# Gathered rows in the pooled channels' buffer, four homes for expert outputs, another order for the first five expert tiles

## The chip, the cores and the metric

One Trainium2 chip, one of its cores. The core has five engines with queues of their own: TensorE (PE, matrix products; PEld is its loading of weights), VectorE (DVE), ScalarE (ACT), GpSimd (POOL) and SyncE (SP, which mostly starts transfers). They run side by side and meet only at semaphores; each works through its own instructions in program order. The metric is the device time of one execution in microseconds (us). The clock of TensorE has two levels here, 1.2 and 2.4 GHz; PEclk 0.50 and 1.00 in the rows.

## The reference

`x` is (4, 1024, 192). B = 4 sequences; after the pooling each has N = 512 tokens of D = 192 channels, 2048 tokens in all.

```python
h = pool_max2(relu(pointwise(depthwise_conv7(x))))           # 4 x 512 x 192
h = layernorm(real(fft2(h))) * gamma + beta
n = layernorm(h); q, k, v = n @ Wq.T, n @ Wk.T, n @ Wv.T     # 12 heads of 16
h = h + causal_taylor_attention(q, k, v) @ Wo.T              # weights 1 + s + s*s/2
x2 = layernorm(h)
probs = softmax(x2 @ Wg + bg)                                # 8 experts, the best one each
y = expert_e(x2) = gelu(x2 @ W1[e] + b1[e]) @ W2[e] + b2[e]  # 192 -> 768 -> 192
ffn = y * max(probs)
v = clip(ffn @ Wv + bv); scores = sigmoid(x2 @ Wm + bm)
mask = scores among the 204 highest of its sequence
feats = diag((tridiag(v) - i)^-1) * mask                     # scan along the tokens
out = h + ffn + bk_scale * (feats @ Wo + bo)
```

## The kernel before, in words

The sequences go one after the other through convolution, Fourier transform, projection and attention. Then come the experts. Tokens are sorted by expert into 23 tiles of 128 slots (`SLOT_TILES`), each tile with one expert. The places of the tokens are found in two passes: pass 0 for sequences 0 to 2 while the attention of sequence 3 still runs, pass 1 for sequence 3, whose rows `x2` exist only after its attention is projected and normalised. Pass 0 fills tiles 0 to 4 (`SURE` = 5) for certain; tile 5 and later need pass 1.

One slot tile takes these steps:

- GpSimd `gather(i)` (L619): an indirect transfer brings 128 rows of `x2` from DRAM into `xs[i % 2]`.
- TensorE `turn_slots(i)` (L1640, L1641) transposes them into PSUM; ScalarE `copy_slots(i)` (L766) copies them to `xsT`.
- VectorE `fetch_w1(i)` (L1127, L1128, L1134) copies the expert's first weights (the 768 wide part, the pair part of 384) and its bias out of the tables of all experts. It reads the expert's number with a register load first.
- TensorE `up(i)` (24 products, L1650 and L1654), ScalarE `gelu(i)` (6 activations, L774), TensorE `down(i)` (6 products, shown as 12 records, L1664) into the one bank `att[2]`.
- VectorE `copy_out(i)` takes the result out of `att[2]` (L1148), weighs it (L1151) and sums it with `Wv` (L1154). GpSimd `store_slots(i)` (L629) scatters it to DRAM.

`down(i)` waits until tile i-1 has been taken out of `att[2]` (`ys_copied`), `up(i)` until `xsT` is copied (`xst_copied`) and gelu i-2 is done. The outputs have two homes `ys`; `copy_out(i)` waits until tile i-2 is stored.

Around the seam between attention and experts, TensorE's order is written by hand: `find_tokens(0)` (L1564), `turn_attended` (L1488, L1490), `turn_back` (L1409, L1413), `output` of the last sequence (L1421, L1424), with short groups of idle products between them (`keep_clock`, L1346), then slot tiles 0 and 1, the turning of x2 (`turn`, L1550), `down(0)`, `logits` (L1574), and so on up to a loop over pairs of tiles that begins with `up(5)`. The second pass on VectorE is `choose(1)` (L980 to L990), `place(1)` (L1003 to L1060), `name_tiles(1)` (L1100 to L1104: experts of the tiles, `te_ready`) and `name_slots(1)` (L1069 to L1075: token of each slot, `slots_named`).

`xs`, `ys` and `hT` share the buffer `probs`, whose first 768 columns also hold the attention result that `turn_back` reads. So `gather(0)` waits for `back_done`:

```python
if i == 0:
    pool.wait_ge(s_saved, 32 * (B - 1))
    pool.wait_ge(slots_named, 1)
    pool.wait_ge(back_done, 2 * B)
```

## Time and profile before

| | us |
|---|---|
| median of 3 runs | 426.69 |
| the runs | 425.43 to 428.47 |
| profiled execution, its own time | 426.79 |
| its span, first to last instruction | 425.0 |

| engine | busy us | share of the span |
|---|---|---|
| PE | 379.0 | 89% |
| DVE | 281.1 | 66% |
| ACT | 160.5 | 38% |
| POOL | 103.0 | 24% |

The chain that ended last runs over PE for 57% of the span and over DVE for 24%. By time the run has these parts: convolution to the last attention, 0 to about 255 us; the seam with the first expert tiles, 255 to 304 us; the loop over expert tiles, 304 to about 383 us; the scan, the features and the stores, to 425 us. A share over the whole span says little here: the change touches only the second part, and there the question is what each engine waits for.

In the rows, the start is in us from the beginning of the span, then the duration; a bracket is the idle time ahead and what ended it. `issue` there stands for time for which the profile shows no releaser. Several like instructions in a row are merged, with their count.

### The profile page before, as it was taken

Reading aid. Unit: us, or ns where it says so; the run is one execution under the profiler, and the core shown is the slowest. Engines: PE = TensorE matmul, PEld = TensorE weight load, DVE = VectorE, ACT = ScalarE, POOL = GpSimd, SP = SyncE. Lnnn points to the kernel's source line nnn. Section 1 sums busy time; section 2 is a strip of 40 time slices with the busy share of each in tenths; the row PEclk is TensorE's granted clock in tenths of the full one; section 3 lists DMA queues with packets and bytes.
Section 4 is the critical chain, followed back from the end, with each engine's and each line's share of the span. In section 5 each row is a group of like instructions: output and inputs, shape, how many; then the busy total and the mean of one; then the engine's idle time right before and its main releaser. Section 6 shows DMA issues by size and latency. Waiting matters only on the chain.

```text
span 425.0 us, 7812 instructions
## 1 busy us (share of the span) xinstructions
PE 379.0 (89%) x2658; PEld 255.4 (60%) x2659; DVE 281.1 (66%) x901; ACT 160.5 (38%) x321; POOL 103.0 (24%) x154
## 2 busy tenths in 40 slices
PE   8999899799998998989998899995899999997273
PEld 4476547133673364723677228894899999996252
DVE  4589734899688995986433853664446656657783
ACT  1001131595317843187531781471243443441000
POOL 2000030151303612045300260310543443421000
PEclk9999899699999999999995799997899999999656
DMA  8664049400685015810279705310411112112504
GB/s 266 194 197 149 0 123 258 126 3 2 191 217 149 2 38 155 217 52 2 68 209 291 333 20 202 129 35 9 164 43 56 45 53 56 43 40 54 169 1 148
DMA packets 26900, 47.94 MB, mean 113 GB/s; under 512 B 11044, under 2 KB 21860, under 8 KB 25332
## 3 DMA queue, kind: packets, MB, share of 16 engines
q1 hardware_dynamic: 21412, 32.73, 25.0%
q10 hardware_dynamic: 2288, 7.15, 6.4%
q0 software_dynamic: 3168, 7.65, 6.2%
q8 instruction: 17, 0.28, 0.3%
q14 instruction: 15, 0.12, 0.1%
HBM read 36.84 MB, written 10.68 MB: 112 GB/s over the span
## 4 chain that ended last, share of the span: by engine, by line
PE 57%; DVE 24%; DMA 6%; issue 5%; ACT 4%; POOL 2%; DVEq 1%; SPq 0%; ACTq 0%; POOLq 0%
PE att L1664 10%; PE ring L1650 8%; PE ring L1654 5%; PE att L1527 4%; PE ring L1515 4%; ACT probs L674 3%; DMA w1b<-q_parts 3%; DVE wide L824 2%; PE att L1490 2%; POOL probs L603 2%; PE att L1581 2%; PE ring L1395 1%; PE ring L1361 1%; DVE stats L833 1%; PE ring L1400 1%
## 5 line engine op out<-in xcount | busy, mean ns | idle before, releaser
L674 ACT ACTIVATE probs<-ring,ones 128x1024 f32<-128x1024 f32 (+2 forms) x72 | 66.3, 970 | 15.9 <-PE ring L1515 14.5
L603 POOL TENSOR_SCALAR_AFFINE_SELECT probs<-probs 128x256 f32<-128x256 f32 (+1 forms) x72 | 40.7, 569 | 111.6 <-ACT probs L674 111.4
L1664 PE MATMUL att<-w,probs 128*128 x276 | 50.6, 335 | 3.3 <-DVE probs L1148 3.3
L1664 PEld LDWEIGHTS att<-w,probs 128*128 128x128 f32 x276 | 45.8, 195 | 4.2 <-issue 4.1
L1515 PE MATMUL ring<-w1b 128*128 128x512 bf16 (+3 forms) x192 | 40.6, 324 | 6.5 <-ACT probs L674 3.6
L824 DVE SCALAR_TENSOR_TENSOR wide<-w,wdw,wide 128x512 f32<-128x512 f32 x60 | 44.1, 779 | 0.8
L1527 PE MATMUL att<-probs,va 128*32 128x512 f32 (+3 forms) x384 | 39.8, 454 | 2.4 <-POOL probs L603 1.8
L629 POOL DMA_INDIRECT ffn_by_token<-probs,target_i x23 | 23.1, 1002 | 52.6 <-DVE probs L1154 44.7
L1515 PEld LDWEIGHTS ring<-w1b 128*128 128x128 bf16 x192 | 13.1, 101 | 37.8 <-ACT probs L674 26.5
L774 ACT ACTIVATE probs<-ring,q_area 128x128 f32<-128x128 f32 x72 | 19.9, 375 | 38.1 <-DVE k_area L1127 13.5
L619 POOL DMA_INDIRECT probs<-x_by_token,source_i x23 | 22.6, 984 | 41.4 <-issue 16.7
L1148 DVE TENSOR_TENSOR probs<-att,oT 128x192 f32<-128x192 f32 x23 | 8.2, 358 | 31.8 <-PE att L1664 30.0
L774 ACT ACTIVATE probs<-ring,k_area 128x128 f32<-128x128 f32 x66 | 18.2, 375 | 26.3 <-PE ring L1654 23.7
L467 POOL DMA_DIRECT2D k_parts<-k_area x12 | 6.9, 578 | 82.3 <-ACT k_area L707 77.7
L1346 PE MATMUL att<-idle 128*128 128x256 bf16 x172 | 25.0, 314 | 1.2 <-POOL idle L578 1.2
L1346 PEld LDWEIGHTS att<-idle 128*128 128x128 bf16 x172 | 19.0, 113 | 7.8 <-issue 2.9
L1527 PEld LDWEIGHTS att<-probs,va 128*32 128x32 f32 x384 | 8.2, 108 | 22.3 <-POOL probs L603 18.1
L1650 PE MATMUL ring<-xsT,q_area 128*128 128x128 f32 x144 | 19.2, 285 | 1.7 <-issue 1.7
L1650 PEld LDWEIGHTS ring<-xsT,q_area 128*128 128x128 f32 x144 | 17.4, 196 | 2.7 <-issue 2.1
L1650 PE MATMUL ring<-xsT,k_area 128*128 128x128 f32 x132 | 17.4, 282 | 0.6 <-ACT xsT L766 0.6
L1650 PEld LDWEIGHTS ring<-xsT,k_area 128*128 128x128 f32 x132 | 15.6, 191 | 1.9 <-issue 0.8
L857 DVE TENSOR_REDUCE pooled<-ring 128x512 f32<-128x1024 f32 x4 | 4.9, 1226 | 17.7 <-PE ring L1365 12.9
(369 smaller groups left out, 713.7 us busy)
## 6 DMA issues: line engine op xcount, KB each, us to landing
w1b<-k_parts ACTq DMA_DIRECT2D x16, 384.0 KB, 9.8
w1b<-q_parts SPq DMA_DIRECT2D x16, 384.0 KB, 9.1
w<-in_w SPq DMA_DIRECT2D x1, 4608.0 KB
w1a<-in_w1a SPq DMA_DIRECT2D x1, 3072.0 KB, 10.3
w<-in_x SPq DMA_DIRECT2D x4, 512.0 KB, 3.5
w<-in_x SPq DMA_DIRECT2D x8, 256.0 KB, 5.0
q_parts<-q_area SPq DMA_DIRECT2D x12, 128.0 KB, 2.6
k_parts<-k_area POOLq DMA_DIRECT2D x12, 128.0 KB, 2.6
```

Of the source, the lines that this page charges most:

```text
L603: nc.gpsimd.affine_select(diag, diag, [[0, len(UNITS[n][1])], [1, P]], ALU.is_ge, minus_one, base=0, channel_multiplier=-1).then_inc(p_rea ...
L619: nc.gpsimd.indirect_dma_start(xs[slot], None, known, bass.IndirectOffsetOnAxis(source_i[:, i:i + 1], 0)).then_inc(s_xs[slot], 16)
L629: nc.gpsimd.indirect_dma_start(ffn_dram, bass.IndirectOffsetOnAxis(target_i[:, i:i + 1], 0), ys[slot], None).then_inc(s_ys[slot], 16)
L674: nc.scalar.activation(squares(n), bank[:, :, 0:N - P * j], ACT.Square, bias=ones[:, 0:1], scale=0.25).then_inc(sq_done, 1)
L774: nc.scalar.activation(hT[slot][:, c, :], ring[slot][:, c % 2, P * (c // 2):P * (c // 2) + P], ACT.Gelu_apprx_tanh, bias=b1_col[slot][:, c ...
L824: ins = nc.vector.scalar_tensor_tensor(dst, src, w, dst, ALU.mult, ALU.add)
L1346: nc.tensor.matmul(bank[:, 0:2 * P], idle[:, 0:P], idle[:], start=True, stop=True)
L1515: last = nc.tensor.matmul(bank[:, at, 0:N - P * j], k_stack[:, h, P * j:P * j + P], q_stack[:, h, P * j:N], start=True, stop=True)
L1527: last = nc.tensor.matmul(att[g][QUAD * q:QUAD * q + QUAD, P * j:N], va[:, j, h, :], squares(n)[:, at, :], start=(j == 0), stop=(j == 1))
L1650: nc.tensor.matmul(out[c], w1_wide[slot][:, P * c:P * c + P], xsT[slot][:, 0, :], start=(c < 2), stop=False)
L1654: last = nc.tensor.matmul(out[c], w1_pair[slot][rows, P * (c // 2):P * (c // 2) + P], xsT[slot][rows, 1, :], start=False, stop=(c >= HC - 2))
L1664: last = nc.tensor.matmul(att[2][:, 0:D], hT[slot][:, c, :], w2[:, bass.ds((e * HC + c) * D, D)], start=(c == 0), stop=(c == HC - 1))
```

## The change

- `xs`, the gathered rows, moves from `probs` to `pooled`, the buffer of the pooled channels, which is free once the last Fourier transform is done. `gather(0)` now waits for `row_done` in place of `back_done`. `ys` has four homes (`YS`), each with its own semaphore; `hT`, behind them in `probs`, begins 386 columns further on.
- TensorE: slot tiles 0 and 1 are turned ahead of `output`; of 14 idle products around `output`, 2 are left, ahead of it. Tiles 2 and 3 are turned ahead of x2 (`turn`), each before or behind an `up`. `down(2)` moves ahead of `up(4)`, `down(3)` and `down(4)` ahead of the transpose of the scores; tiles 5 and 6 go up before `down(5)`, and the loop starts one pair later.
- VectorE: `first_weights()` fetches the wide weights and the biases of tiles 0 and 1 during the last attention, ahead of `name_slots(0)`; only the pair parts stay where all was. `copy_out` is cut in `take_out` (the copy out of PSUM, L1148 before) and `weigh_out` (L1151, L1154). Tile 1 is taken out, and tile 4's bias fetched, in the middle of `place(1)`; tile 2 directly behind it; `name_slots(1)` comes ahead of `name_tiles(1)`, tile 3 is taken out behind both. The weighing of 1 to 3 and the copy of the scores come later, between the fetches for tiles 5 and 6.
- ScalarE: tiles 2 and 3 are copied ahead of `gelu(1)`; tile 4 is copied ahead of `gelu(3)`, and `gelu(4)` and tile 5 follow ahead of its loop.
- GpSimd: `gather(5)` and `gather(6)` come directly behind `store_slots(0)`.

```diff
-        xs = [probs[:, 2 * P * i:2 * P * i + 2 * P] for i in range(2)]
+        xs = [pooled[:, i, 0:2 * P] for i in range(2)]
         at = 2 * 2 * P
-        ys = [probs[:, at + (D + 1) * i:at + (D + 1) * (1 + i)] for i in range(2)]
-        at += 2 * (D + 1)
+        ys = [probs[:, at + (D + 1) * i:at + (D + 1) * (1 + i)] for i in range(YS)]
+        at += YS * (D + 1)
...
+        def outs_stored(eng, tiles):
+    for i in range(YS):
+        eng.wait_ge(s_ys[i], 16 * len(range(i, tiles, YS)))
...
-            pool.wait_ge(back_done, 2 * B)
+            pool.wait_ge(row_done, B)
...
     for i in range(SURE):
         gather(i, i % 2)
     pool.wait_ge(s_vzero, 16)
-    for i in range(SLOT_TILES):
-        store_slots(i, i % 2)
+    store_slots(0)
+    gather(SURE, SURE % 2)
+    gather(SURE + 1, (SURE + 1) % 2)
+    store_slots(1)
+    for i in range(2, SLOT_TILES):
+        store_slots(i)
         if i + SURE < SLOT_TILES:
             gather(i + SURE, (i + SURE) % 2)
...
     copy_slots(0, 0)
     copy_slots(1, 1)
     gelu(0, 0)
+    copy_slots(2, 0)
+    copy_slots(3, 1)
     gelu(1, 1)
     turned(B - 1)
-    copy_slots(2, 0)
-    copy_slots(3, 1)
     exponents(1)
     nc.scalar.activation(score[:], lg[:, :, E], ACT.Sigmoid).then_inc(sc_ready, 1)
     gelu(2, 0)
-    with act.Fori(1, TILE_PAIRS - 1) as i:
+    copy_slots(4, 0)
+    gelu(3, 1)
+    gelu(4, 0)
+    copy_slots(5, 1)
+    with act.Fori(2, TILE_PAIRS - 1) as i:
...
             name_tiles(0)
+            first_weights()
             name_slots(0)
...
         st.then(V.tensor_tensor(tile_of(excl), tile_of(excl), wide_e(here), ALU.add))
+        if halfway is not None:
+            halfway()
         pre = misc[:, 2 * P:2 * P + w].rearrange("p (t e) -> p t e", e=E)
...
+    def first_weights():
+        dve.wait_ge(te_ready, 1)
+        dve.wait_ge(s_w1a, 16)
+        dve.wait_ge(s_part_out[0], 16 * 2 * PARTS * B)
+        dve.wait_ge(s_part_out[1], 16 * 2 * PARTS * B)
+        for i in range(2):
+            fetch_wide(i, i, expert_of(i))
+        for i in range(2):
+            fetch_bias(i, i, expert_of(i))
...
+    def take_out(i):
+        e = expert_of(i)
+        ahead(dve, s_ys[i % YS], 16 * (i // YS))
         dve.wait_ge(dn_done, i + 1)
-        out = ys[slot][:, 0:D]
+        out = ys[i % YS][:, 0:D]
         V.tensor_tensor(out, att[2][:, 0:D], b2[:, bass.ds(e * D, D)], ALU.add
                         ).then_inc(ys_copied, 1)
+
+    def weigh_out(i):
+        out, v = ys[i % YS][:, 0:D], ys[i % YS][:, D:D + 1]
...
     dve.wait_ge(s_w1b, 16)
-    fetch_w1(0, 0)
-    fetch_w1(1, 1)
+    for i in range(2):
+        fetch_pair(i, i, expert_of(i))
     add_attended(B - 1)
     normalise_again(B - 1)
     fetch_w1(2, 0)
     fetch_w1(3, 1)
     dve.wait_ge(s_w2, 32)
-    copy_out(0, 0, 0)
+    copy_out(0)
     choose(1)
     fetch_w1(4, 0, bias=False)
-    place(1)
+
+    def second_out():
+        take_out(1)
+        fetch_bias(4, 0, expert_of(4))
+
+    place(1, second_out)
+    take_out(2)
+    name_slots(1)
     name_tiles(1)
-    name_slots(1)
-    fetch_bias(4, 0, dve.value_load(te_i[0:1, bass.ds(4, 1)], min_val=0, max_val=E - 1))
+    take_out(3)
     dve.wait_ge(te_ready, 2)
-    for i in range(1, SLOT_TILES - 1):
-        copy_out(i, i % 2, i // 2)
-        if i > 1 and i + 3 < SLOT_TILES:
+    fetch_w1(5, 1)
+    weigh_out(1)
+    weigh_out(2)
+    fetch_w1(6, 0)
+    weigh_out(3)
+    dve.wait_ge(st_done, 1)
+    V.tensor_copy(score_t[:], misc[0:TT, 2 * P:3 * P]).then_inc(st_copied, 1)
+    st.then(V.memset(qq[:, 0:2, :, :, :], 0.0))
+    st.mark(V.memset(qq[:, 1, :, 0, 0:1], 1.0))
+    st.mark(V.memset(qq[:, 0, :, 0, 1:2], 1.0))
+    st.mark(V.memset(neg_pos[:, 0:1], -GROUP_SCALE))
+    st.mark(V.memset(neg_pos[:, 1:2], GROUP_SCALE))
+    for i in range(4, SLOT_TILES - 1):
...
     turn_attended(B - 1)
-    keep_clock(6, ring[1][:, 0, :])
+    keep_clock(6)
     turn_back(B - 1)
-    keep_clock(6, ring[1][:, 0, :])
-    output(B - 1)
-    keep_clock(8, ring[0][:, 1, :])
...
-        pe.wait_ge(w1_fetched, 3 * i + 2)
+        pe.wait_ge(w1_fetched, 5 + i if isinstance(i, int) and i < 2 else 3 * i + 2)
...
     turn_slots(0, 0, 1)
     turn_slots(1, 1, 1)
+    keep_clock(2)
+    output(B - 1)
     up(0, 0)
+    pe.wait_ge(attn_added, B)
+    turn_slots(2, 0, 2)
     up(1, 1)
-    pe.wait_ge(attn_added, B)
+    turn_slots(3, 1, 2)
+    pe.wait_ge(xst_copied, 4)
     turn(B - 1)
     pe.wait_ge(te_ready, 1)
     pe.wait_ge(s_w2, 32)
     down(0, 0)
     pe.wait_ge(t2_copied, B)
-    turn_slots(2, 0, 2)
-    turn_slots(3, 1, 2)
     logits(B - 1)
     up(2, 0)
     count(1)
     down(1, 1)
     up(3, 1)
     turn_slots(4, 0, 3)
+    down(2, 0)
     up(4, 0)
     find_tokens(1)
+    down(3, 1)
+    down(4, 0)
     pe.wait_ge(sc_ready, 1)
     pe.wait_ge(slots_named, 2)
     nc.tensor.transpose(misc[0:TT, 2 * P:3 * P], score[:], ident[:]).then_inc(st_done, 1)
-    down(2, 0)
-    down(3, 1)
     pe.wait_ge(te_ready, 2)
     turn_slots(5, 1, 3)
-    with pe.Fori(2, TILE_PAIRS - 1) as i:
+    up(5, 1)
+    turn_slots(6, 0, 4)
+    up(6, 0)
+    turn_slots(7, 1, 4)
+    down(5, 1)
+    with pe.Fori(3, TILE_PAIRS - 1) as i:
```

How the instructions stand on three engines follows; the line number at the start of a row is that of its own kernel.

TensorE at the seam, from the idle products behind `turn_attended` to the first `up`; `pooled` and, of before, `probs` with `ident` into `ring1` are the slot tiles, `wo` the projection. Before:

```order
L1346 MATMUL ring1<-idle 128x256 x6
L1409 MATMUL ring0<-ident,probs 128x128 x4
L1413 MATMUL ring0<-ident,probs 64x128 x4
L1346 MATMUL ring1<-idle 128x256 x6
L1421 MATMUL att<-wo,probs 128x192 x4
L1424 MATMUL att<-wo,probs 128x192 x4
L1346 MATMUL ring0<-idle 128x256 x8
L1640 MATMUL ring1<-ident,probs 128x128
L1641 MATMUL ring1<-ident,probs 128x128
L1640 MATMUL ring1<-ident,probs 128x128
L1641 MATMUL ring1<-ident,probs 128x128
L1650 MATMUL ring0<-xsT0,q_area 128x128 x6
```

And now:

```order
L1392 MATMUL att<-idle 128x256 x6
L1455 MATMUL ring0<-ident,probs 128x128 x4
L1459 MATMUL ring0<-ident,probs 64x128 x4
L1683 MATMUL ring1<-ident,pooled 128x128
L1684 MATMUL ring1<-ident,pooled 128x128
L1683 MATMUL ring1<-ident,pooled 128x128
L1684 MATMUL ring1<-ident,pooled 128x128
L1392 MATMUL att<-idle 128x256 x2
L1467 MATMUL att<-wo,probs 128x192 x4
L1470 MATMUL att<-wo,probs 128x192 x4
L1693 MATMUL ring0<-xsT0,q_area 128x128 x6
L1697 MATMUL ring0<-xsT0,q_area 128x128 x6
```

The two slot tiles moved ahead of the projection, and `up(0)` follows it at once.

ScalarE from the table load for gelu on; `xsT0` and `xsT1` are the copies of even and odd slot tiles, `x2T` the turned x2, `probs<-ring` a gelu. Before:

```order
L766 ACTIVATE xsT0<-ring1 128x256
L766 ACTIVATE xsT1<-ring1 128x256
L774 ACTIVATE probs<-ring0,q_area 128x128 x6
L774 ACTIVATE probs<-ring1,k_area 128x128 x6
L755 ACTIVATE x2T<-att 96x1024
L766 ACTIVATE xsT0<-att 128x256
L766 ACTIVATE xsT1<-att 128x256
L747 ACT_TABLE_LOAD
```

And now:

```order
L773 ACTIVATE xsT0<-ring1 128x256
L773 ACTIVATE xsT1<-ring1 128x256
L781 ACTIVATE probs<-ring0,q_area 128x128 x6
L773 ACTIVATE xsT0<-att 128x256
L773 ACTIVATE xsT1<-att 128x256
L781 ACTIVATE probs<-ring1,k_area 128x128 x6
L762 ACTIVATE x2T<-att 96x1024
L754 ACT_TABLE_LOAD
```

The copies of tiles 2 and 3 moved ahead of `gelu(1)` and of `x2T`.

VectorE in the second pass; `te_i` with the ISA rows behind it is the register load of an expert's number. Before, the end of that stretch, with `name_slots(1)`, the bias of tile 4 and the taking out of tile 1:

```order
L1072 TENSOR_SCALAR source_i<-held 128x18
L1073 SCALAR_TENSOR_TENSOR spare_row<-held,dump_tab 128x18
L1075 SCALAR_TENSOR_TENSOR target_i<-held,spare_row 128x18
L1194 TENSOR_LOAD te_i
L1194 ISA x2
L1134 ISA
L1134 COPY q_area<-b1t 128x6
L1144 TENSOR_LOAD te_i
L1144 ISA x2
L1148 ISA
L1148 TENSOR_TENSOR probs<-att,oT 128x192
```

And now the middle of `place(1)`:

```order
L1045 TENSOR_TENSOR excl<-excl,et 128x32
L1138 TENSOR_LOAD te_i
L1138 ISA x2
L1184 ISA
L1184 TENSOR_TENSOR probs<-att,oT 128x192
L1138 TENSOR_LOAD te_i
L1138 ISA x2
L1166 ISA
L1166 COPY q_area<-b1t 128x6
L1049 TENSOR_TENSOR key<-excl,misc 128x32
```

The taking out of tile 1 and the bias moved between the two halves of `place(1)`.

## Rows read from the trace of the kernel before

**Rows 1.** Stretches of the run: busy time per engine, PEclk, DMA share and GB/s.
```profile
79.00:80.00 1.00, 0.59 (x2) 0.13 (x2) 0.86 (x5) 1.00 (x2) 0.40 (x1) 0.50 1.00 393
...
230.00:235.00 5.00, 3.82 (x17) 2.91 (x17) 1.71 (x7) 1.11 (x1) 0.35 (x1) 0.50 1.01 356
...
291.00:292.00 1.00, 1.00 (x11) 1.00 (x12) 0.00 (x0) 0.00 (x0) 0.00 (x0) 0.50 0.00 0
...
305.00:350.00 45.00, 45.00 (x375) 41.59 (x373) 25.29 (x82) 18.93 (x70) 19.94 (x21) 1.00 0.18 52
```
**Rows 2.** Chain of work that ended last: start, us, engine, line.
```profile
313.83 1.44 PE ring L1650 x12
```
**Rows 3.** Timeline, TensorE: start, us, operation, count, [idle before and its releaser].
```profile
77.54 1.34 PE L1515 MATMUL ring<-w1b 128*128 128x512 bf16 x4 [2.08 <-DMA w1b<-q_parts]
...
267.60 1.05 PE L1346 MATMUL ring<-idle 128*128 128x256 bf16 x8
...
269.87 1.50 PE L1650 MATMUL ring<-xsT,q_area 128*128 128x128 f32 x12
...
272.17 1.60 PE L1650 MATMUL ring<-xsT,k_area 128*128 128x128 f32 x12
...
274.57 1.08 PE L1550 MATMUL att<-ident,x_all 128*96 128x128 f32 x8
275.49 2.12 PE L1664 MATMUL att<-w,probs 128*128 x12
...
277.88 1.85 PE L1574 MATMUL misc<-wgm,x2T 96*128 96x9 f32 x16
...
288.91 2.13 PE L1650 MATMUL ring<-xsT,q_area 128*128 128x128 f32 x12 [1.71 <-issue]
...
296.98 3.69 PE L1664 MATMUL att<-w,probs 128*128 x12 [1.82 <-DVE probs L1148]
```
**Rows 4.** Timeline, ScalarE, from the last projection's copy to gelu 3.
```profile
264.38 0.81 ACT L689 ACTIVATE probs<-ring 128x768 f32<-128x768 f32 x1 [8.30 <-PE ring L1413]
...
266.50 0.20 ACT L761 ACTIVATE warm<-ones 128x1 f32<-128x1 f32 x1
...
286.88 1.65 ACT L774 ACTIVATE probs<-ring,k_area 128x128 f32<-128x128 f32 x6 [1.63 <-PE ring L1654]
288.39 0.42 ACT L766 ACTIVATE xsT<-att 128x256 f32<-128x256 f32 x1
```
**Rows 5.** Timeline, VectorE, from the first slot table to the second output.
```profile
258.35 0.20 DVE L1067 COPY held<-misc 128x46 f32<-128x46 f32 x1 [7.97 <-PE misc L1564]
...
265.10 0.56 DVE L1127 COPY k_area<-w1a 128x768 f32 x1
...
273.81 0.15 DVE L953 COPY nz<-x_all 128x1 f32<-128x1 f32 x1
...
285.61 0.21 DVE L1035 TENSOR_TENSOR key<-excl,misc 128x32 f32<-128x32 f32 x1
...
289.49 0.34 DVE L1100 TENSOR_TENSOR y<-te,et 1x192 f32<-1x192 f32 x1
...
290.44 0.16 DVE L1104 TENSOR_SCALAR te_i<-te 1x19 int32<-1x19 f32 x1
...
294.56 0.18 DVE L1075 SCALAR_TENSOR_TENSOR target_i<-held,spare_row 128x18 int32<-128x18 f32 x1
...
296.47 0.36 DVE L1148 TENSOR_TENSOR probs<-att,oT 128x192 f32<-128x192 f32 x1 [0.97 <-issue]
```
**Rows 6.** Timeline, GpSimd: attention's masks, first gather, gather of tile 5.
```profile
252.34 0.64 POOL L603 TENSOR_SCALAR_AFFINE_SELECT probs<-probs 128x512 f32<-128x512 f32 x1 [0.39 <-ACT probs L674]
...
265.20 1.36 POOL L619 DMA_INDIRECT probs<-x_by_token,source_i  x1 [10.66 <-PE ring L1413]
...
295.49 0.98 POOL L619 DMA_INDIRECT probs<-x_by_token,source_i  x1 [14.84 <-issue]
```
**Rows 7.** Gathers of 255 to 310 us, start to landing, minimum, median, maximum.
```profile
DMA to landing us min/median/max: 2.7/2.8/2.9
```

53 lines of the change are left out of this document (24 added, 29 removed).

## The prediction

> **What bounds the kernel now.** I first read the windows by stage. In the loop over expert tiles TensorE is busy 45.00 of 45 us at full clock, VectorE 25.29 [rows 1]. The change alters no instruction inside that loop but the addresses of `xs`, `ys` and `hT`, so the loop keeps its length, and I ask only when it reaches a common point. The chain has one: `up(7)` begins at 313.83 [rows 2], with all `up` to 6 and all `down` to 5 behind it. In the changed order `up(7)` is the first operation of the loop, with the same work behind it. Whatever this point gains, the end gains.
>
> Ahead of it, TensorE's timeline shows the price of one operation [rows 3]: `up` 2.30 us (269.87 to 272.17), `turn` 0.92 (274.57 to 275.49), `down(0)` with two slot tiles 2.39 (275.49 to 277.88), which is 1.95 and twice 0.22, logits 1.7. A row's own duration overlaps the next by about 0.15. From `up(0)` at 269.87 to `up(7)` at 313.83 are 43.96 us. The work in it is 7 `up` (16.1), 6 `down` (11.7), 6 slot tiles (1.3), `turn`, logits and small products (4.1): 33.2 us. So 10.8 us are idle time and half clock: 1.71 ahead of `up(4)` and 1.82 ahead of `down(2)` are two of the gaps, and `down(2)` takes 3.69 in place of 2.12 [rows 3].
>
> **The change step by step**, on the clock of the profiled run.
>
> *Gathers.* The slot table is begun at 258.35 and takes four dependent operations of 0.2 [rows 5]: ready at 259.1. `gather(0)` now needs nothing more. Tile 5's gather began 0.75 after its table (294.74 to 295.49) [rows 5, 6], so it starts at 259.85 in place of 265.20, and lands 2.8 later [rows 7], at 262.7; the second follows 1.66 behind (1.36 plus 0.3) and lands at 264.3. TensorE ends `turn_back` at about 264.35, when ScalarE's copy begins (264.38) [rows 4]. The slot tiles fit there (to 264.8), since `output` has to wait for that copy until 265.19 anyway. What is queued behind a late gather now is `output`, and behind that x2: the cover is 0.4 us, after it each late microsecond counts in full.
>
> *Up(0).* The eight idle products behind `output` began at 267.60, `up(0)` came at 269.87, after a wait for the second gather [rows 3]. Now it starts at 267.6: ScalarE ends its table load and trial at 266.70 [rows 4] and copies tile 0 by 267.1. Gain 2.3.
>
> *To x2.* `up(0)` to 269.9, slot tile 2, `up(1)` to 272.4, slot tile 3 to 272.65. Then `turn` waits for x2, whose last operation VectorE does at 273.81, to 273.96 [rows 5]. Nothing in the change moves it. `turn` starts at 274.1, before 274.57: of the 2.3 us, 0.46 are left, and TensorE has a new gap of 1.45 us. As two slot tiles are out of the way, the logits end 0.9 earlier, at 278.7.
>
> *Second pass.* VectorE is 0.9 earlier up to the middle of `place(1)`: 284.7 in place of 285.61 [rows 5]. There the change adds `take_out(1)` (0.36), tile 4's bias (0.17) and a register load for each. The load's price has no row of its own; the nearest is the gap of 0.97 ahead of `copy_out(1)` [rows 5], which may hold waits too. Bounds 0 and 0.97; I take 0.6, nearer to the row. That is 1.7 us, and the second half of `place(1)` is 3.9 (285.61 to 289.49) [rows 5]: positions at 290.4, before 289.5. The operations of 1 to 3 that are cut out come back later; they are hidden, as `down` of tile 4 waits only for taking out.
>
> *Tiles 2 to 4.* TensorE: `up(2)` to 281.0, count to 281.5, `down(1)` to 283.5, `up(3)` to 285.8, slot tile 4 to 286.0, `down(2)` to 288.0, `up(4)` to 290.3. Before, `up(4)` waited 1.71 for a copy that stood behind `gelu(3)`: ScalarE did that gelu from 286.88 and the copy from 288.39 to 288.81 [rows 4]. Now the copy stands ahead of the gelu and `down(2)` fills the time. `find_tokens(1)` waits for positions to 290.6 and takes 0.9; `down(3)` to 293.5. VectorE names slots by 292.4, tiles by 293.6 (1.1, from 289.49 to 290.60) [rows 5], takes out tile 3 by 294.55 with one register load. `down(4)` runs 294.7 to 296.7, after a gap of 1.2.
>
> *Tiles 5 to 7.* `gather(5)` starts 0.75 after 292.4 and lands by 296.0, hidden. Slot tile 5 is turned at 296.9 and copied by 297.5; `up(5)` 297.7 to 300.0, slot tile 6 to 300.2. `up(6)` now stands directly behind, and its copy behind `gelu(5)`: 1.65 for the gelu and 0.42 for the copy [rows 4], so it starts at 302.3, a gap of 2.1. `up(6)` to 304.6, slot tile 7 and `down(5)` to 306.8, `up(7)` at 306.95. That is 6.9 us ahead of 313.83: 2.3 ahead of `up(0)` and 4.6 out of the 10.8, of which 6.1 remain.
>
> *First weights ahead of time.* Two wide copies of 0.56 and two small ones fall into the 7.97 us in which VectorE waited for the slot table [rows 5]. If that cover were gone, about 3 us of them with register loads would stand ahead of `gather(0)`. They lie beside the last masks on GpSimd. The first gather's instruction, beside such copies (265.10), took 1.36; tile 5's, with VectorE still, 0.98 [rows 5, 6]. So a mask may take 0.4 longer, 0.8 for two; each had 0.39 idle ahead of it [rows 6], so I take 0 and keep 0.8 for the range. The Trainium skill, "SBUF — State Buffer", section "Who interferes with whom", says that VectorE in its two-port mode and GpSimd fully block one another; the two rows bear it out in direction. By the skill's rule each wide copy would hold a mask for up to its 0.56, 1.1 us in all, and the time would be 422.6.
>
> *Four homes.* No store is waited for before, by these rows. Nothing is won in the loop.
>
> *The clock.* TensorE fell to half clock in the three cases here in which it had idled so long: 2.08 ahead of 77.54, and 0.50 at 79; 1.71 ahead of 288.91, and 0.50 at 291; 1.82 ahead of `down(2)`, which then took 3.69 [rows 1, 3]. The new gap of 2.1 ahead of `up(6)` is of that kind. A stay at half clock costs what `down(2)` shows, 3.69 less 2.12, 1.6 us; an `up` shows 2.13 for 1.50 in its first half [rows 3], so 1.3 for both. The gap of 1.45 is shorter than these three, but `turn` and logits follow. I count one fall: 6.9 less 1.6 is 5.3, and 426.79 less 5.3 is 421.5. The profiled execution (426.79) stands 0.1 above the median, so this needs no shift. The Trainium skill, "TensorE: Matmul & The Clock Gate", section "HAM oscillation — how this bites in real kernels", would have only longer gaps than these do harm. By that the 2.1 us gap costs nothing, which is the first rival; the rows of this trace speak against it.
>
> **The rivals.** *No fall of the clock*: 419.9. For it, before lost one stay to a gap of 1.71 and one to 1.82, and the clock may look at a luckier moment; against it, three of three gaps.
>
> *Two falls*: also after 1.45 us. `down(0)`, the logits and `up(2)` then run slowly; one stay costs 1.6, and two in a row, if the logits don't lift it, 3. It gives 423.1 to 424.5. For it: at 230 to 235 the clock was still 0.50 with TensorE busy 3.82 of 5 us [rows 1].
>
> *VectorE becomes the limit of tiles 2 to 4*: each register load costs 0.97 in place of 0.6, and the loads stand on the way to the slot table and to `down(4)`. Four of them add 1.5, in all 423.0.
>
> *The change doesn't do what it says*: the early gathers are worth 0.66 of waiting, x2 comes when it came, and what the new order fills on TensorE comes back as waits for gelu and for taking out. Then 0.46 remains: 426.3.
>
> *Slower*: the clock falls at the 1.45 us gap and stays low through the sparse stretch up to the loop, as it did from about 225 to past 235 [rows 1]. From 276 to 302, 3 `up` more at 1.3 and 4 `down` more at 1.6, 1.9 for the logits and 0.5 for the rest make about 13 less what hides in the gaps (2), so 11: 6.9 are lost and 4 more, near 431. It decides once half clock lasts some 15 us.
>
> **How the numbers follow.** Forecast 0.38, no fall 0.15, two falls 0.25, VectorE 0.09, no effect 0.07, slower 0.06. The likeliest is 421.5, with its own range 420.3 to 422.6 (masks 0.8 and register loads up, shorter gaps down). From no fall, with 0.6 below it, to two falls with 0.5 above: 419.3 to 425.0; outside are the last two cases and a part of the edges. Over 1% is 4.27 us, about what a measurement of this kernel can tell from no change. Faster than that, under 422.4: no fall, nine tenths of the forecast and a little of two falls, 0.56. Slower than 431.0: half of the last case and other harm not named, 0.05. The rest, 0.39, is within 1%.
>
> **What would show it.** `up(0)` within 0.3 us of the end of `output`; x2's last operation at the same time; a gap of about 1.4 us ahead of `turn`, about 2 ahead of `up(6)` and 0.50 behind it; `up(4)` at full clock directly behind `down(2)`; slot table two at about 292.4; `up(7)` near 308.5. The sum is wrong if `output` waits for the slot tiles, if the masks stretch the last attention, or if the loop's period changes.

## The result

| | before | changed |
|---|---|---|
| median of 20 runs, us | 428.76 | 425.71 |
| the runs, us | 425.43 to 432.63 | 423.22 to 430.99 |
| profiled execution, its own time | 426.79 | 424.41 |
| its span | 425.0 | 422.5 |
| changed to before, 95% interval | | 0.9946 (0.9925 to 0.9967) |

The changed kernel is 0.5% faster, 2.3 us (1.4 to 3.2 by the interval). The medians of all runs lie 3.05 us apart; the ratio is formed from fast runs alone, without the few in the slower state that executions on this chip can fall into. Forecast were 421.5 us and 5.3 us of gain. Two things hide in the difference. The three runs of before that the forecast started from were low ones: the median of 20 is 2.1 us above theirs. And of the gain, more than half is missing; where it went is the question of the rest.

How the parts of the two executions stand, from the start of `find_tokens(0)` on TensorE to the starts of `up(0)`, `up(7)` and `up(22)`, the last tile's, and to the end, in us:

| | before | changed |
|---|---|---|
| `find_tokens(0)` to `up(0)` | 14.5 | 12.2 |
| `up(0)` to `up(7)` | 43.8 | 44.2 |
| `up(7)` to `up(22)` | 69.0 | 68.9 |
| `up(22)` to the end | 42.3 | 42.4 |

I call the first two together *the seam*: 58.3 before, 56.4 changed. The loop and what follows kept their length. In the seam the time up to `up(0)` fell by the 2.3 forecast, and nothing came of the 3.0 more (4.6 less 1.6 of half clock) that was to come behind it; that part is even 0.4 longer.

TensorE of the changed kernel in the seam (timeline; the line numbers are its own: L1470 is the end of `output`, L1693 and L1697 are `up`, L1683 and L1684 a slot tile, L1596 `turn`, L1707 `down`; the last row is the beginning of `up(7)`, cut off by the edge of the view), which answers to [rows 3]:

```profile
266.17 0.92 PE L1470 MATMUL att<-wo,probs 64*128 64x192 f32 x8
267.02 1.60 PE L1693 MATMUL ring<-xsT,q_area 128*128 128x128 f32 x12
...
273.50 1.05 PE L1596 MATMUL att<-ident,x_all 128*96 128x128 f32 x8 [1.06 <-ACT xsT L773]
...
287.81 1.50 PE L1693 MATMUL ring<-xsT,q_area 128*128 128x128 f32 x12
...
291.03 2.20 PE L1707 MATMUL att<-w,probs 128*128 x12
294.15 2.21 PE L1707 MATMUL att<-w,probs 128*128 x12 [0.93 <-DVE probs L1184]
...
297.21 1.58 PE L1693 MATMUL ring<-xsT,k_area 128*128 128x128 f32 x12 [0.52 <-issue]
298.72 0.94 PE L1697 MATMUL ring<-xsT,k_area 64*128 64x128 f32 x12
...
299.76 0.27 PE L1684 MATMUL att<-ident,pooled 128*128 128x128 f32 x1
304.06 2.90 PE L1693 MATMUL ring<-xsT,q_area 128*128 128x128 f32 x12 [4.03 <-DVE k_area L1166]
306.89 1.65 PE L1697 MATMUL ring<-xsT,q_area 64*128 64x128 f32 x12
308.47 0.47 PE L1683 MATMUL att<-ident,pooled 128*128 128x128 f32 x1
...
311.23 0.94 PE L1693 MATMUL ring<-xsT,k_area 128*128 128x128 f32 x7
```

Up to 299.76 it goes as forecast: `up(0)` right behind `output`, a gap of 1.06 ahead of `turn`, `up(4)` at full clock behind `down(2)`, a gap of 0.93 ahead of `down(4)`, `up(5)` 0.52 behind its slot tile. Then come 4.03 us of nothing ahead of `up(6)` where 2.1 were forecast, and behind it `up(6)` takes 4.4 us (304.06 to 308.47) in place of 2.4, and `down(5)` is stretched too.

The releases show that the gap is not ScalarE's doing alone. ScalarE in that stretch (timeline; L781 is gelu, L773 the copy of a slot tile):

```profile
296.73 0.38 ACT L773 ACTIVATE xsT<-att 128x256 f32<-128x256 f32 x1 [4.51 <-issue]
302.03 1.66 ACT L781 ACTIVATE probs<-ring,k_area 128x128 f32<-128x128 f32 x6 [4.91 <-remote]
303.54 0.42 ACT L773 ACTIVATE xsT<-att 128x256 f32<-128x256 f32 x1
```
VectorE's and GpSimd's first instructions behind the gap (L1142 is the copy of the next weights, L622 the next gather):

```profile
302.13 0.56 DVE L1142 COPY k_area<-w1a 128x768 f32 x1 [1.11 <-remote]
302.31 1.24 POOL L622 DMA_INDIRECT pooled<-x_by_token,source_i  x1 [1.24 <-remote]
```
The granted clock around it (windows, columns as in [rows 1]):

```profile
302.00:303.00 1.00, 0.00 (x0) 0.00 (x0) 0.83 (x2) 0.97 (x4) 0.69 (x1) 0.88 1.00 328
306.00:309.00 3.00, 3.00 (x20) 2.55 (x20) 0.00 (x0) 0.36 (x2) 0.00 (x0) 0.50 0.00 1
309.00:310.00 1.00, 1.00 (x6) 1.00 (x6) 0.00 (x0) 1.00 (x6) 0.57 (x1) 0.70 0.00 0
```

`gelu(5)` waits for the last product of `up(5)`, whose record ends at 299.66, and begins at 302.03, with `remote` as its releaser: the wait ended with a signal that belongs to no record ending near it. VectorE's copy of the next weights (302.13) and GpSimd's next gather (302.31), which wait for `up(5)` and for slot tile 6, go on within 0.3 us of it, after 1.11 and 1.24 of idle time marked `remote`. The trace also holds the times of the signals themselves. That of `up(5)` is recorded at 302.00 and that of slot tile 6 at 302.05, 2.34 and 2.02 us after the ends of the products' records (299.66, 300.03); of the 309 signals of TensorE in this trace the median comes 0.01 after its record. So all three engines got TensorE's signals some 2 us late by the records. I call these *the late signals*. The ends of TensorE's records are modelled by the profile, so whether the products themselves ended late or only their signals is not shown. The mean clock of 0.88 in 302 to 303 and of 0.70 in 309 to 310 puts the fall at 302.8 and the rise at 309.6: 6.8 us at half clock.

### The profile page after: what moved, and what is told of

Same layout as the page of the kernel before. It is cut to its first block and busy times, and to the rows that moved or that the text cites. A ratio compares the mean times of both kernels' runs of the same rounds, so it can differ in the third digit from the quotient of the medians.

```text
span 422.5 us, 7775 instructions
## 1 busy us (share of the span) xinstructions
PE 374.3 (89%) x2642; PEld 252.8 (60%) x2647; DVE 281.7 (67%) x901; ACT 160.3 (38%) x321; POOL 103.3 (24%) x154
## 5 line engine op out<-in xcount | busy, mean ns | idle before, releaser
L1707 PE MATMUL att<-w,probs 128*128 x276 | 49.5, 330 | 1.8 <-DVE probs L1184 1.7
L1707 PEld LDWEIGHTS att<-w,probs 128*128 128x128 f32 x276 | 44.7, 192 | 2.8 <-issue 2.7
L1561 PE MATMUL ring<-w1b 128*128 128x256 bf16 (+3 forms) x188 | 39.5, 321 | 7.5 <-ACT probs L681 3.5
L781 ACT ACTIVATE probs<-ring,q_area 128x128 f32<-128x128 f32 x72 | 19.9, 374 | 31.7 <-PE ring L1697 13.5
L622 POOL DMA_INDIRECT pooled<-x_by_token,source_i x23 | 22.9, 993 | 36.8 <-issue 20.6
L781 ACT ACTIVATE probs<-ring,k_area 128x128 f32<-128x128 f32 x66 | 18.2, 376 | 26.5 <-PE ring L1697 19.0
L1392 PE MATMUL att<-idle 128*128 128x256 bf16 x180 | 25.9, 310 | 1.2 <-POOL idle L581 1.2
L1693 PE MATMUL ring<-xsT,q_area 128*128 128x128 f32 x144 | 20.0, 292 | 4.0 <-DVE k_area L1166 4.0
L1693 PEld LDWEIGHTS ring<-xsT,q_area 128*128 128x128 f32 x144 | 18.3, 203 | 5.1 <-issue 4.5
L1693 PE MATMUL ring<-xsT,k_area 128*128 128x128 f32 x132 | 17.2, 280 | 0.5 <-issue 0.5
L1693 PEld LDWEIGHTS ring<-xsT,k_area 128*128 128x128 f32 x132 | 15.7, 191 | 1.6 <-issue 0.7
```

The costliest lines, as they stand in the source:

```text
L622: nc.gpsimd.indirect_dma_start(xs[slot], None, known, bass.IndirectOffsetOnAxis(source_i[:, i:i + 1], 0)).then_inc(s_xs[slot], 16)
L781: nc.scalar.activation(hT[slot][:, c, :], ring[slot][:, c % 2, P * (c // 2):P * (c // 2) + P], ACT.Gelu_apprx_tanh, bias=b1_col[slot][:, c ...
L1392: nc.tensor.matmul(bank[:, 0:2 * P], idle[:, 0:P], idle[:], start=True, stop=True)
L1561: last = nc.tensor.matmul(bank[:, at, 0:N - P * j], k_stack[:, h, P * j:P * j + P], q_stack[:, h, P * j:N], start=True, stop=True)
L1693: nc.tensor.matmul(out[c], w1_wide[slot][:, P * c:P * c + P], xsT[slot][:, 0, :], start=(c < 2), stop=False)
L1707: last = nc.tensor.matmul(att[2][:, 0:D], hT[slot][:, c, :], w2[:, bass.ds((e * HC + c) * D, D)], start=(c == 0), stop=(c == HC - 1))
```

## The experiments

Each kernel's own seam, from its trace, is the measure, since the totals scatter more. The time to the start of `find_tokens(0)` varied from 253.2 to 260.3 us over twenty traces of code that is the same up to there but for the first weights. The first 250 us show what goes with it, TensorE's granted clock (the column behind the busy times). The changed kernel unchanged, in its last trace (`again_e`):

```profile
0.00:250.00 250.00, 229.37 (x1542) 125.72 (x1543) 180.20 (x512) 104.31 (x146) 55.39 (x105) 0.96 0.48 138
```
And with a later store of the scores (`scores_late`):

```profile
0.00:250.00 250.00, 226.73 (x1476) 124.69 (x1481) 175.68 (x497) 98.74 (x139) 54.40 (x98) 0.94 0.47 138
```

By my estimate 0.96 against 0.94 of 250 us is 5 us of clock, and the starts of `find_tokens(0)` were 253.7 and 260.3. A difference of 2 us between two single times says nothing about an edit behind it.

### The changed kernel again, three variants of the place ahead of up(6)

Run unchanged:

> The changed kernel once more, so that the variants below have a partner on the same chip. Its first trace has up(6) at 304.06, 4.03 us after slot tile 6, and ScalarE, VectorE and GpSimd all go on at 302.0 to 302.3 although TensorE's records of up(5) end at 299.66. Theory A (belongs to this order of work): the stop comes again within 0.3 us, ratio to before 0.994. Theory B (an accident of one execution): the gap ahead of up(6) is 2.1 us, and the ratio nearer 0.99.

It gave 424.28 us (median of 4), ratio 0.9885 (0.9807 to 0.9963), and a seam of 53.06 us in place of 56.44: 5.3 us less than before, which is the forecast gain to a tenth. The interval of these 4 runs holds the first ratio too, so it is the trace that tells them apart. A later trace (`again_e`, below) has the same course; TensorE in it:

```profile
296.13 1.58 PE L1693 MATMUL ring<-xsT,k_area 128*128 128x128 f32 x12 [0.52 <-issue]
...
300.65 1.79 PE L1693 MATMUL ring<-xsT,q_area 128*128 128x128 f32 x12 [1.70 <-issue]
302.37 1.65 PE L1697 MATMUL ring<-xsT,q_area 64*128 64x128 f32 x12
...
306.81 1.50 PE L1693 MATMUL ring<-xsT,k_area 128*128 128x128 f32 x12
```
ScalarE of the same trace:

```profile
298.63 1.65 ACT L781 ACTIVATE probs<-ring,k_area 128x128 f32<-128x128 f32 x6 [2.59 <-PE ring L1697]
300.14 0.42 ACT L773 ACTIVATE xsT<-att 128x256 f32<-128x256 f32 x1
```
And its windows with the granted clock:

```profile
301.00:302.00 1.00, 1.00 (x10) 1.00 (x10) 0.27 (x2) 0.00 (x0) 0.69 (x2) 0.94 0.79 295
303.00:304.00 1.00, 1.00 (x11) 0.78 (x9) 0.00 (x0) 0.00 (x0) 0.00 (x0) 0.50 0.83 293
305.00:306.00 1.00, 1.00 (x7) 1.00 (x7) 0.00 (x0) 1.00 (x4) 0.90 (x1) 0.86 0.08 31
```

Here `gelu(5)` (298.63) begins when `up(5)` ends, the gap ahead of `up(6)` (300.65) is 1.70, and by the windows half clock lasts from 301.9 to 305.3, 3.4 us. So the missing 3.35 us of the first trace are two terms: 2.33 more of gap, and 1.0 more of half clock, since the longer stay covers all of `up(6)` and reaches into `down(5)` (`up(6)` to `up(7)` is 7.17 there, 6.16 here).

ScalarE copies slot tile 6 ahead of `gelu(5)`:

```diff
             copy_slots(5, 1)
-            with act.Fori(2, TILE_PAIRS - 1) as i:
+            copy_slots(6, 0)
+            gelu(5, 1)
+            gelu(6, 0)
+            copy_slots(7, 1)
+            with act.Fori(3, TILE_PAIRS - 1) as i:
```

> ScalarE copies slot tile 6 ahead of gelu(5), in place of behind it, and its loop begins one pair later. Theory A (order): what is lost ahead of up(6) is ScalarE's gelu and copy and the half clock behind the gap: up(6) comes within 0.7 us of slot tile 6 and at full clock, up(7) 4 to 5 us earlier, ratio to before 0.984. Theory B (signals of TensorE are held up by something else for 2.3 us at this time): up(6) still comes 2.5 us or more after slot tile 6, half clock stays, ratio about 0.99.

421.36 us, ratio 0.9842 (0.9753 to 0.993), seam 50.33. Against the unchanged kernel beside it (53.06) that is 2.7 us; the 4 to 5 expected were reckoned from the first trace, with its late signals. Its second run is shown below.

TensorE does 14 idle products in the gap, begun when tile 4 has been taken out:

```diff
             turn_slots(6, 0, 4)
+            pe.wait_ge(ys_copied, 5)
+            keep_clock(14)
             up(6, 0)
```

> 14 idle products (1.5 us) are put into the gap ahead of up(6), behind the taking out of tile 4. Theory A (clock): up(6) takes 2.3 in place of 4.4 us and down(5) 1.95, so up(7) comes 2 to 2.7 us earlier at the same start of up(6); ratio 0.989. Theory B (the gap alone counts, or the idle products end too soon): up(6) stays at 4.4 us, ratio 0.994.

421.52 us, ratio 0.9833 (0.9762 to 0.9903), seam 51.6. The same kernel in a later trace, `warm_gap_b`:

> Idle products of TensorE in the gap ahead of up(6), which begin when take_out of tile 4 has been copied. Without late signals 51.6 us as once before. With them: if the signals are late because TensorE itself stands still, the idle products stand still too and the way is about 2.3 us longer, 53.9 us, with or without a half clock behind; if only the signals' way is held up, the products run through and the clock stays at 2.4 GHz.

```profile
299.60 1.58 PE L1693 MATMUL ring<-xsT,k_area 128*128 128x128 f32 x12 [0.52 <-issue]
...
302.14 0.27 PE L1684 MATMUL att<-ident,pooled 128*128 128x128 f32 x1
302.69 1.70 PE L1392 MATMUL att<-idle 128*128 128x256 bf16 x14 [0.28 <-DVE probs L1184]
304.23 1.50 PE L1693 MATMUL ring<-xsT,q_area 128*128 128x128 f32 x12
```

Single time 421.91 us, seam 51.55. `up(6)` stands where it stood within 0.1 us, 4.63 behind `up(5)`, but runs its first half in 1.50; the stay at half clock is gone and `up(6)` to `up(7)` is 4.53 in place of 6.16. So a fall of the clock behind a gap of 1.7 us costs 1.5 to 1.6, as the forecast took it from `down(2)` of before, and it was the gap that brought it. The Trainium skill, "TensorE: Matmul & The Clock Gate", section "HAM oscillation — how this bites in real kernels", lets only longer gaps than this do harm; no trace here with a gap of 1.70 us ahead of `up(6)` was spared (seven), and both with idle products in it were.

The store of the scores, which is on its way while `up(5)` runs, held back until `up(7)`:

```diff
             sp.wait_ge(st_copied, 1)
+            sp.wait_ge(up_done, 8)
```

> SyncE holds back the store of the scores and their spreading to all partitions (1 MB) until up(7) is done. Theory A (these transfers hold up the signals): ScalarE begins gelu(5) at once behind up(5), the gap ahead of up(6) is 2.1 in place of 4.0 us, ratio 0.990. Theory B (they don't): the gap stays 4.0, ratio 0.994 or a little more, if the count of higher scores now waits.

426.59 us, ratio 0.9952 (0.9915 to 0.999), seam 53.07. The second and third trace, with their expectations:

> The changed kernel with the store of the scores held back until up(7), for a second trace. If the score store, which is on its way while up(5) runs, is what delays TensorE's signals, there is no late signal here either and the way from find_tokens(0) to up(7) is 53.1 us again. If the late signals come whatever the scores do, there is a good half chance of 56.4 us.

> The score store held back until up(7), on this chip. Two traces of it on a chip without late signals say nothing on the cause. If this chip shows them in the unchanged kernel (56.4 us): the theory that the score store, which is under way at that moment, delays TensorE expects none here and 53.1 us; the rival (TensorE's own stop at this place of the program) expects 56.4 us again. On a chip without late signals both expect 53.1 us. From up(7) to up(22) 72.1 us rather than 68.9 as in both traces, since the comparisons of the scores then start later.

Seams 53.11 and 53.06. All three are without the late signals, but so were all other kernels that ran beside them. The edit has a price of its own, 3.2 us: from `up(7)` to `up(22)` all three traces take 72.1 to 72.2 us, not 68.9. TensorE of `scores_late_c` shows where:

```profile
318.84 2.21 PE L1708 MATMUL att<-w,probs 128*128 x12 [2.88 <-DVE probs L1185]
```
VectorE of the same trace:

```profile
317.40 0.75 DVE L1173 TENSOR_SCALAR_CACHE_REDUCE y<-wide,score 128x512 f32<-128x512 f32 x1 [5.96 <-DMA wide<-scores_linear]
...
318.23 0.36 DVE L1185 TENSOR_TENSOR probs<-att,oT 128x192 f32<-128x192 f32 x1
```

VectorE waits 5.96 us for the scores to come back from DRAM, the taking out of tile 7 (L1185, 318.23) is queued behind, and TensorE stands 2.88 us ahead of its next `down`. The store in its early place is thus needed.

### The gather's wait put back

```diff
-                    pool.wait_ge(row_done, B)
+                    pool.wait_ge(back_done, 2 * B)
```

> One part undone alone: the first gather waits for back_done again, as before, but TensorE's order stays as changed, with slot tiles 0 and 1 ahead of the projection. Theory A (the early gather is what makes the new order possible, and its cover is small): both gathers land 3.4 to 5.2 us behind turn_back, the projection waits for them from 264.8 on, x2 and all behind it come about 4.5 us later; ratio to the kernel before 1.003. Theory B (the gathers don't matter, x2 comes when it came): no change, ratio 0.992.

It ran beside two runs of before and one of the changed kernel:

> The kernel before once more, for a second trace. So far the changed kernel's three traces have 53.1, 53.1 and (with the stop) 56.4 us from the first product behind the attention, find_tokens(0), to up(7); the one trace of before has 58.3. Theory A (the stage gained what was forecast, 5.3, and the whole lost some elsewhere): before again has 57.8 to 58.8 in that stage, and what differs lies ahead of find_tokens(0). Theory B (the first trace of before was unlucky in its clock): the stage takes 55 to 57 here.

> A third trace of the kernel before, for the same question, above all for when the last attention ends: 255.4 in the first trace; the changed kernel's traces have 254.8 to 260.3. Theory A (the masks or the early weights make the attention end later): about 255.4 again. Theory B (this point moves by some us from execution to execution in both kernels): anything from 254 to 261.

> The changed kernel, one more trace: 53.1 us from find_tokens(0) to up(7) and a gap of 1.9 us ahead of up(6), if the stop of the first trace was an accident; 56.4 and 4.0 if it is common.

429.37 us, ratio 1.0041 (0.9995 to 1.0087). TensorE at the seam:

```profile
261.55 0.66 PE L1459 MATMUL ring<-ident,probs 128*64 128x128 f32 x8
265.93 0.33 PE L1683 MATMUL ring<-ident,pooled 128*128 128x128 f32 x1 [3.72 <-DMA pooled<-x_by_token,source_i]
...
267.21 0.48 PE L1683 MATMUL ring<-ident,pooled 128*128 128x128 f32 x1 [0.84 <-DMA pooled<-x_by_token,source_i]
...
268.12 2.63 PE L1467 MATMUL att<-wo,probs 128*128 128x192 f32 x8
```

The transfers now land 3.72 and 0.84 us after TensorE is ready, `output` is queued behind them, and its first half takes 2.63 in place of 1.57. From `find_tokens(0)` to `up(0)` it is 18.3 in place of 12.2, and the seam 61.27 against 56.45 of `again_b` on the same chip: 4.8 worse, and 3 worse than before. Up to `up(0)` it is 6.1 worse; 1.2 come back behind the gap of 4.06 ahead of `up(6)`, where this trace stays at half clock for 3.4 us and not for 6.8 (`up(6)` to `up(7)` 5.93, not 7.16). Both traces have the late signals, which before has not, and the interval of the ratio holds 1. So the new order on TensorE pays only with the rows in `pooled`; without them its gain is gone, and whether it would be a loss is not shown.

`again_b` took 425.05 us and has the late signals (seam 56.45), and `gather_late` has them too. The two runs of before took 432.08 and 427.18 us with seams of 61.19 and 58.44. In the first the stay at half clock that begins in the gap ahead of `down(2)` lasts 10.2 us, where the other three traces of before have 3.4, without any edit; so before can lose there as well.

### The first weights put back

```diff
                     name_tiles(0)
-                    first_weights()
                     name_slots(0)
...
             divide(B - 1)
+            first_weights()
             dve.wait_ge(s_w1b, 16)
```

> The changed kernel, but VectorE brings the first two wide weight halves and biases after the last division again, not among the masks. In the changed kernel that block ran from 249.84 to 253.64, 3.8 us. Placed behind the division (end 262.7) it would end at about 265.9, the two narrow halves about 1.8 us later at 267.8; up(0), which started at 267.02, needs the first narrow half (about 267.0), so it moves by 0 to 0.2; add_attended, which started at 267.14, moves to 267.8, and the turn of x2 with it. Theory (the early weights are worth what they take off this path): about 0.7 us slower than the changed kernel from find_tokens(0) to up(7). Rival (the block in front cost as much ahead of the attention's end, where it delayed the masks): the attention ends up to 3.8 us earlier and the whole is 1 to 3 us faster than the changed kernel. Second rival (nothing hangs on it): the same within 0.3 us.

422.36 us, ratio 0.9919 (0.9876 to 0.9963); seam 53.62 against 53.05 of the unchanged kernel beside it (`again_c`). The 0.57 us are 0.1 ahead of `up(0)` and the gap ahead of `turn`, 1.54 in place of 1.06. The clock did not fall behind this longer gap either; TensorE (timeline):

```profile
272.96 1.05 PE L1596 MATMUL att<-ident,x_all 128*96 128x128 f32 x8 [1.54 <-issue]
```

The block is worth 0.6 us behind the attention, near the 0.7 expected. The contention that the forecast kept 0.8 us for is there, and it fell on both engines in turn. In the changed kernel, VectorE (timeline):

```profile
250.85 0.95 DVE L1142 COPY q_area<-w1a 128x768 f32 x1 [1.05 <-issue]
251.72 0.55 DVE L1142 COPY k_area<-w1a 128x768 f32 x1
```
And GpSimd's masks beside it:

```profile
250.75 0.63 POOL L606 TENSOR_SCALAR_AFFINE_SELECT probs<-probs 128x512 f32<-128x512 f32 x1 [0.39 <-ACT probs L681]
251.77 0.99 POOL L606 TENSOR_SCALAR_AFFINE_SELECT probs<-probs 128x512 f32<-128x512 f32 x1 [0.39 <-ACT probs L681]
```

The first wide copy began behind a mask and took 0.95 instead of 0.55, while that mask took the 0.63 it takes elsewhere. The second wide copy took its 0.55, and the mask that began 0.05 behind it took 0.99. The Trainium skill, "SBUF — State Buffer", section "Who interferes with whom", would have the two engines block one another; the rows agree in size, and each time the one that began later waited. It cost nothing here: `find_tokens(0)` begins 3.02 us after this last long mask in all twenty traces, with a mask of 0.99 as with one of 0.64, such as `weights_late` and the kernel before have.

### Is it the execution, the order or the chip?

> The changed kernel, unchanged, for one more trace of the gap ahead of up(6). Of three traces so far two have TensorE's signals of up(5) about 2.3 us late, a gap of 4.0 us and a way of 56.4 us from find_tokens(0) to up(7), and one has none, a gap of 1.9 us and 53.1 us. The theory that the late signals are a matter of the execution expects one or the other of these two values, nothing between.

424.28 us, seam 53.05, no late signals.

> The kernel with ScalarE's copy of slot tile 6 ahead of gelu(5), once more, to narrow its interval. If the order of ScalarE at this place is what TensorE waited for, the ratio to the kernel before is again 0.984 (0.975 to 0.993) and the way from find_tokens(0) to up(7) again near 50.3 us. If the first result was a lucky execution, the ratio lies near that of the changed kernel, 0.9946, and the way near 53 to 56 us.

419.94 us, ratio 0.9883 (0.9828 to 0.9937), seam 50.33. TensorE in it:

```profile
300.09 0.27 PE L1688 MATMUL att<-ident,pooled 128*128 128x128 f32 x1
300.88 1.58 PE L1697 MATMUL ring<-xsT,q_area 128*128 128x128 f32 x12 [0.52 <-issue]
...
305.49 0.71 PE L1697 MATMUL ring<-xsT,k_area 128*128 128x128 f32 x4
```

(The last row is cut off by the edge of the view.) Gap 0.52, no fall. The 2.73 us that it gains on 53.06 are 1.18 of gap and 1.55 of clock.

> The changed kernel unchanged, with five rounds. Of its order at up(5) there are eight traces from one chip, none with late signals of TensorE, and two from another chip, both with them (again_b, gather_late); the way from find_tokens(0) to up(7) is 53.06 us in the first and 56.45 in the second. Theory (the late signals go with the chip): on a chip without them the way is 53.06 us and the ratio to the kernel before is 1 - 5.3/428 = 0.988 (0.985 to 0.991); on a chip with them 56.45 and 1 - 1.9/428 = 0.9955 (0.993 to 0.998). Rival (they go with the single execution): both values in traces of one chip, and a ratio between.

425.87 us, ratio 0.9964 (0.9928 to 1.0), seam 56.39, late signals.

> The kernel with ScalarE's copy of slot tile 6 ahead of gelu(5), beside the one above on the same chip. Without late signals the way is 50.33 us as twice before. On a chip with them the theory has TensorE's signals of up(5) late here too: the copy of slot tile 6 then waits, up(6) starts about 2.3 us later with a gap near 2.9 us instead of 0.5, a half-clock window follows (1.7 us and more), and the way is 53 to 56 us; against the changed kernel it would still gain about 1 to 3 us.

424.21 us, ratio 0.9928 (0.9888 to 0.9967), seam 53.92. The late signals hit this order too: 2.31 and 1.98 us behind the ends of the records. TensorE:

```profile
301.76 0.27 PE L1688 MATMUL att<-ident,pooled 128*128 128x128 f32 x1
304.52 2.51 PE L1697 MATMUL ring<-xsT,q_area 128*128 128x128 f32 x12 [2.49 <-issue]
```
ScalarE of the same trace:

```profile
304.04 0.39 ACT L773 ACTIVATE xsT<-att 128x256 f32<-128x256 f32 x1 [4.92 <-remote]
304.32 1.65 ACT L781 ACTIVATE probs<-ring,k_area 128x128 f32<-128x128 f32 x6
```

ScalarE begins the copy of slot tile 6, which was turned at 302.0, at 304.04 (`remote`), the gap is 2.49 and half clock follows. Against the changed kernel on the same chip it still gains 2.5 us by the seams.

> The changed kernel once more, to tell of which kind this chip is. With late signals of TensorE after up(5) (two of three chips so far) the gap ahead of up(6) is 4.0 us and the way from find_tokens(0) to up(7) 56.4 us; without them 1.7 to 1.9 us and 53.06 us.

420.44 us, seam 53.09, no late signals, on the chip on which `again_d` and `copy6_c` had them.

> The kernel before on this chip. Of the same stage 58.3 and 58.4 us so far (61.2 in one trace with two more half-clock windows), without a late signal of TensorE. The theory that the late signals belong to the changed order expects 58.3 to 58.4 here on a chip of either kind.

428.03 us, seam 58.20.

All together, with the sets of kernels that ran one after the other on a chip, the seams of their traces, and what these seams would make of the ratio (1 plus the seam less the 58.3 of before, and 3.2 more for the late store, over 428.3, about the median of before). Where a kernel was timed, a set has 4 to 20 runs of it; each kernel of a set has one trace:

| set, chip | late signals | kernel | seam | ratio by the seam | ratio measured |
|---|---|---|---|---|---|
| 1 | yes | changed | 56.44 | 0.9957 | 0.9946 (0.9925 to 0.9967) |
| 2, chip 4 | no | changed | 53.06 | 0.9878 | 0.9885 (0.9807 to 0.9963) |
| | | copy ahead | 50.33 | 0.9814 | 0.9842 (0.9753 to 0.993) |
| | | idle products | 51.6 | 0.9844 | 0.9833 (0.9762 to 0.9903) |
| | | scores late | 53.07 | 0.9953 | 0.9952 (0.9915 to 0.999) |
| 3, chip 12 | yes | changed | 56.45 | | |
| | | gather late | 61.27 | 1.0069 | 1.0041 (0.9995 to 1.0087) |
| 4, chip 4 | no | changed | 53.05 | | |
| | | weights late | 53.62 | 0.9891 | 0.9919 (0.9876 to 0.9963) |
| | | copy ahead | 50.33 | 0.9814 | 0.9883 (0.9828 to 0.9937) |
| 5, chip 1 | yes | changed | 56.39 | 0.9955 | 0.9964 (0.9928 to 1.0) |
| | | copy ahead | 53.92 | 0.9898 | 0.9928 (0.9888 to 0.9967) |
| 6, chip 1 | no | changed | 53.09 | | |
| | | idle products | 51.55 | | |

In a set, either every trace of the new order has the late signals or none has: five traces with, eleven without, no exception. Chip 1 had a set of each kind, so it is not the chip alone. The timed runs bear it out as far as their intervals reach (one of the ten leaves out what the seam says, and only just): the changed kernel's three timed sets stand near 0.988 without and 0.995 to 0.996 with. The order with the copy ahead tells it more plainly: medians of 421.36 and 419.94 us without, 424.21 with, while before had 428.01, 428.28 and 428.05 in the same sets.

What differs between the sets I do not know. An instruction fetch it is not: none is recorded between `up(5)` and `up(6)`, in traces of either kind. The store of the scores is neither ruled out nor shown to be the cause. Its packets were through 1.0 us after its issue in both kinds of traces, and its three traces with the later place fell into sets without late signals. But SyncE, which waits for that store's own signal, issued its next transfer 1.50 to 1.67 us after it in four of the five traces with late signals (1.37 in `copy6_c`), and 1.36 to 1.42 in the eleven without. So the hold-up reaches beyond TensorE. In the first trace (SyncE; 1.37 between the same two in `again_e`):

```profile
298.84 0.33 SPq L551 DMA_DIRECT2D scores_linear<-score_t  x1
300.51 0.35 SPq L557 DMA_DIRECT2D wide<-scores_linear  x1
```

And the two kinds of sets differ in one thing more, of both kernels. The traces of sets 1, 3 and 5 hold 4716 to 4748 signals, those of 2, 4 and 6 hold 5062 to 5068; up to 250 us they hold 3006 to 3050, whatever the kind, and the missing ones, most of them signals of transfers, lie behind. Every trace of the new order with the fewer signals has the late ones, no trace with the full number has. Whether what delays the signals also loses records, or the recording itself delays them, is open. The four traces of before, three of them with the fewer signals, have no late signal at this place. No trace with the idle products fell into a set with late signals.

## Why the prediction was right or wrong

- **The loop keeps its length; what `up(7)` gains the end gains**: right. 68.9 against 69.0, and 42.4 against 42.3.
- **Gathers early, cover 0.4 us, `up(0)` right behind `output`, 2.3 us**: right. The first gather began at 259.27, `up(0)` at 267.02, 0.85 behind the start of `output`'s last part. Its undoing cost 4.8.
- **x2 doesn't come earlier, so only 0.46 is kept at `turn`**: right. `turn` came at 273.50; the profiled execution of changed ran 0.6 earlier from the start of the seam, so this is 274.1 on the clock of the forecast. The gap was 1.06, not 1.45, since the two `up` and two slot tiles ahead of it took 5.4 us (267.02 to 272.44) and not 5.05.
- **No fall of the clock behind this gap**: right, in every trace, even behind the 1.54 us of `weights_late`.
- **Second pass with register loads at 0.6**: right within the bounds; VectorE's two cut-in operations have 0.78 and 0.41 us idle ahead of them, 0.6 in the mean:

```profile
285.19 0.36 DVE L1184 TENSOR_TENSOR probs<-att,oT 128x192 f32<-128x192 f32 x1 [0.78 <-DVE excl L1045]
285.96 0.17 DVE L1166 COPY q_area<-b1t 128x6 f32 x1 [0.41 <-issue]
```

  `down(4)` at 294.15 is 294.75 on the forecast's clock (294.7 forecast).
- **First weights beside the masks, taken at 0**: right. One mask took 0.36 longer, as the forecast allowed, and nothing behind it moved.
- **`up(5)` at 297.7, `up(6)` 2.1 behind the slot tile, one fall of 1.6**: `up(5)` right (297.21 and 0.6). The gap and the fall were 1.70 and 1.55 in the sets without late signals, and the seam then 53.06 to 53.09, 5.2 to 5.3 us less than before: the sum holds in full there. The gap was 0.4 shorter because slot tile 6 ended 0.4 later than forecast, so `up(6)` came when it was expected. The sum took 313.83 for the start of `up(7)` before, which TensorE's timeline has at 313.67, so 0.16 of the 6.9 was never there.
- **The step that failed**, "`up(6)` now stands directly behind, and its copy behind `gelu(5)` [...] a gap of 2.1", followed by "I count one fall": it took a signal to arrive when the product's record ends. In the trace of the result the signal of `up(5)` came 2.34 late, the gap was 4.03, and the half clock behind it lasted 6.8 us, not 3.4. Together that is 3.35 us more than in the sets without late signals, leaving 1.9. On the forecast's clock `up(7)` came at 311.83 in place of 308.5. No row of before showed such a delay, and it could have been foreseen only as an unnamed loss; why the signals are late stays open. The rival with two stays in a row (3 us) came near what the doubled stay cost, 2.6 (7.17 less 4.6), but put it behind the gap ahead of `turn`, where the clock never fell.
- **The base**: "stands 0.1 above the median, so this needs no shift" was said of three runs. The median of 20 is 428.76. Two of the 4.2 us between 421.5 and 425.71 are this, and the range, built only of the change's own uncertainties, had no room for it. The other two are less than the 3.35 of the trace; the rest is within the scatter of the runs. Either of the two misses alone would have left the time inside 419.3 to 425.0. That the three runs spread by 3 us should have been read as a warning.

The version with the copy of slot tile 6 ahead of `gelu(5)` is ahead of both kernels: 0.9842, 0.9883 and 0.9928 of before in three sets, each with an interval below 1, and 2.5 to 2.7 us under the changed kernel by the seams. The intervals of the ratios alone do not part it from the changed kernel.
